# Graph attention on one Trainium2 core: attention vectors multiplied into W, the first source lines spread by products, projections and loop in one block, residual product behind the loop

## What is computed

```python
h = (x @ W).reshape(N, H, C)
a_src = jnp.einsum('nhc,hc->nh', h, att_src)
a_dst = jnp.einsum('nhc,hc->nh', h, att_dst)
logits = jax.nn.leaky_relu(a_src[src] + a_dst[dst], NEG_SLOPE)
m = jax.lax.stop_gradient(jax.ops.segment_max(logits, dst, num_segments=N))
e = jnp.exp(logits - m[dst])
s = jax.ops.segment_sum(e, dst, num_segments=N)
alpha = e / s[dst]
msg = h[src] * alpha[:, :, None]
out = jax.ops.segment_sum(msg, dst, num_segments=N).reshape(N, H * C)
out = out + x @ W_res + bias
out = (out - bn_mean) * jax.lax.rsqrt(bn_var + BN_EPS) * bn_gamma + bn_beta
return jax.nn.elu(out)
```

## Time and profile before

| | us |
|---|---|
| median of 3 runs | 3004.32 |
| lowest and highest | 3000.54, 3011.62 |
| the profiled execution's own time | 3009.49 |
| its span, first to last instruction | 3007.7 |
| block before the loop, first transpose to end | 814.4 to 849.2 |
| first logits of the loop | 868.13 |
| end of the loop | 1630.9 |
| first addition of the residual product | 1651.59 |

### The profile page before, as it was taken

One profiled execution on the slowest core, in us unless ns is written; L12 is line 12 of the kernel. 1 busy time (PEld: TensorE's weight loads), 2 busy tenths in 40 slices (PEclk: granted clock), 3 DMA queues, 4 the chain that ended last, 5 costly groups with the idle time before them and its releaser, 6 DMA issues. The chain is left out here.

```text
span 3007.7 us, 59972 instructions
## 1 busy us (share of the span) xinstructions
PE 2511.6 (84%) x19197; PEld 2068.5 (69%) x19197; DVE 2456.1 (82%) x5340; ACT 1962.6 (65%) x3958; POOL 224.6 (7%) x488
## 2 busy tenths in 40 slices
PE   0788888875449888788886599999999999999998
PEld 0555555554447666666664499988998799979997
DVE  7999999953449999899996788877887788868886
ACT  0666666640328888788885477767777677767775
POOL 3000000000000000000000111101110111101110
PEclk9999999987768899899898799999999999999999
DMA  1232332356053233533330243323333234324332
GB/s 43 76 117 107 115 131 92 133 235 164 30 148 109 108 111 121 162 120 112 122 111 27 93 149 133 140 98 130 131 143 137 91 129 149 128 78 143 147 128 86
DMA packets 87376, 355.52 MB, mean 118 GB/s; under 512 B 47453, under 2 KB 59541, under 8 KB 59796
## 3 DMA queue, kind: packets, MB, share of 16 engines
q1 hardware_dynamic: 87149, 352.59, 33.7%
HBM read 285.86 MB, written 65.67 MB: 117 GB/s over the span
## 5 line engine op out<-in xcount | busy, mean ns | idle before, releaser
L1864 ACT ACTIVATE awcol<-aturned 125x500 fp32r<-125x500 f32 (+2 forms) x652 | 373.5, 573 | 310.9 <-PE aturned L1771 307.5
L1961 DVE TENSOR_TENSOR awcol<-aturned,awcol 125x500 fp32r<-125x500 f32 (+2 forms) x652 | 427.7, 656 | 116.4 <-ACT awcol L1864 110.7
L1783 PE MATMUL asum<-awcol,vals_high 125*128 125x512 f32 (+1 forms) x1300 | 477.6, 388 | 0.0
L1366 PE MATMUL gturned<-ident,grow 125*125 125x125 f32 x2500 | 411.2, 306 | 30.1 <-ACT grow L1304 30.1
L1366 PEld LDWEIGHTS gturned<-ident,grow 125*125 125x125 f32 x2500 | 333.7, 205 | 108.5 <-issue 73.1
L1783 PE MATMUL asum<-awcol,vals_low 125*128 125x256 f32 x1300 | 402.8, 319 | 0.0
L1273 DVE SCALAR_TENSOR_TENSOR grow<-line,a_dst 125x3125 f32<-125x3125 f32 x100 | 347.5, 3475 | 38.0 <-DMA line<-lines_dram 25.6
L1304 ACT ACTIVATE grow<-grow,neg 125x3125 f32<-125x3125 f32 x100 | 290.4, 2904 | 125.0 <-DVE neg L1285 125.0
L1282 DVE CUSTOM_DVE_ANT_0 grow<-grow,bias 125x3125 f32<-125x3125 f32 x100 | 341.6, 3416 | 25.7 <-DMA bias<-bias_dram 11.6
L1344 PE MATMUL gparts<-gwcol,h_mem 125*32 125x125 f32 x5000 | 246.1, 292 | 111.4 <-ACT gwcol L1317 111.4
L1317 ACT ACTIVATE gwcol<-gturned 125x1000 f32<-125x1000 f32 x300 | 282.0, 1002 | 16.9 <-PE gturned L1366 16.7
(11 more groups left out here) (305 smaller groups left out, 4874.2 us busy)
## 6 DMA issues: line engine op xcount, KB each, us to landing
abias<-bias_dram SPq DMA_DIRECT2D x100, 1562.5 KB, 6.5
bias<-bias_dram SPq DMA_DIRECT2D x50, 1562.5 KB, 6.5
bias_dram<-lnrow SPq DMA_DIRECT2D x25, 1562.5 KB, 5.2
counts_dram<-pair SPq DMA_DIRECT2D x13, 1562.5 KB, 6.4
pair<-counts_dram SPq DMA_DIRECT2D x13, 1562.5 KB, 16.3
line<-lines_dram SPq DMA_DIRECT2D x8, 1367.2 KB
fixed<-kp SPq DMA_DIRECT2D x250, 4.0 KB, 1.7
agg<-counts_dram SPq DMA_DIRECT2D x2, 1367.2 KB
```

Of the source, the lines that this page charges most:

```text
L1366: last = pe.transpose(bank[q % RING][:, j // 4, j % 4 * T:(j % 4 + 1) * T], row[n % RING][:, t * T:(t + 1) * T], ident[0:T, 0:T])
L1783: last = pe.matmul(sum_ps[e][:, 0:n_cols], left[:, t, :], buffer[:, j * wide:j * wide + n_cols], start=(t == 0 and n == 0), stop=(t == NT ...
L1864: act.activation(operand(P, e, u, 0), turned(P, e, u), ACT.Copy).then_inc(high_copied, 1)
L1961: dve.tensor_tensor(operand(P, e, u, 1), turned(P, e, u), operand(P, e, u, 0).bitcast(FP32), ALU.subtract).then_inc(low_made, 1)
```

## The change

Line numbers of the changed kernel differ: the logits of the loop stand at 1217 instead of 1273, the transposes at 1389 instead of 1366.

- The block `pre` is gone. Its work stands at the head of the loop's block, on the loop's own three double PSUM banks used as six.
- `vcols` is gone. W is turned (128 x 128), multiplied by `att`, and the product `w_att` (128 x 8) meets `cols` directly. `att` is made on VectorE from two loads of 128 elements and the identity.
- The first two source lines (heads 0 and 1) are no longer loaded from device memory. A product whose stationary operand is one column of `w_att`, repeated 125 times, with `cols` as the moving operand gives the line on all 125 partitions; ScalarE copies it, VectorE makes the version times the slope. Heads 2 and 3 are loaded as before.
- `vals` is copied by ScalarE instead of VectorE. The load of ScalarE's Exp table stands ahead of all this.
- The product with the residual matrix is made in the block behind the loop, into seven PSUM banks, and VectorE adds it from there in seven pieces. `cols` stays for that.

```diff
@@ -1110,7 +1110,8 @@
-        res = sbo("res", [T, NT, D])
+        cols = sbo("cols2", [128, N])
+        wres = sbo("wres", [D, D])
...
-        with ExitStack() as pre:
...
-                @block.tensor
-                def _(pe):
-                    pe_turn(pe, banks, "h", h, D, ident)
-                    banks.done(pe, "h")
-                    pe.wait_ge(weights_in, 160)
-                    pe_columns(pe, banks, "vcols", w[:, :], cols)
-                    banks.done(pe, "vcols")
-                    bank = banks.fill(pe, "own", 0)
-                    for t in range(NT):
-                        last = pe.matmul(bank[0:T, 8 * t:8 * t + 8], vcols[:, t * T:(t + 1) * T], att[:, :], start=True, stop=True)
-                    last.then_inc(banks.filled, 1)
-                    pe_rows(pe, banks, "vals", [cols], [w[:, :]])
-                    pe.wait_ge(lines_made, 1)
-                    for k in range(2):
-                        pe.transpose(lines_ps[:, k, :], lines[:, k, :, :].rearrange("p h t -> p (h t)"), ident[0:T, 0:T]
-                                     ).then_inc(lines_ready, 1)
-                    pe_rows(pe, banks, "res", [cols], [wres[:, :]])
...
-                    for name, out in (("vals", vals.rearrange("p t h w -> p t (h w)")), ("res", res)):
-                        for c in range(NC):
-                            ts = tiles_of(c)
-                            bank = banks.full(dve, name, c)
-                            dve.tensor_copy(out[:, ts[0]:ts[-1] + 1, :], rows_view(bank, c, D)).then_inc(banks.read["dve"], 1)
...
+            whole_bank = [loop.enter_context(nc.psum_tensor(f"gturned{r}", [128, 2, 512], FP32)) for r in range(RING)]
+            bank = [whole_bank[r][0:T, :, :] for r in range(RING)]
+            ahead = Banks([whole_bank[r][:, j, :] for r in range(RING) for j in range(2)], sem("l2pre_filled"),
+                          {who: sem(f"l2pre_read_{who}") for who in ("act", "dve")},
+                          [("h", NC, "act"), ("w_turned", 1, "act"), ("w_att", 1, "act"), ("own", 1, "dve"), ("line0", NC, "act"),
+                           ("vals", NC, "act"), ("lines", 1, "act"), ("line1", NC, "act")])
...
-                    load_lines(0, 0)
+                    sp.dma_start(w[:, :], G["L2_gnn_W"]).then_inc(weights_in, 16)
+                    for j, name in enumerate(("L2_gnn_att_src", "L2_gnn_att_dst")):
+                        with nc.allow_non_contiguous_dma(reason="small weights"):
+                            sp.dma_start(att_in[:, j:j + 1], G[name].rearrange("h (c a) -> (h c) a", a=1)).then_inc(weights_in, 16)
+                    sp.dma_start(wres[:, :], G["L2_gnn_W_res"]).then_inc(weights_in, 16)
                     load_bias(0)
                     load_bias(1)
-                    load_lines(0, 1)
+                    ahead.done(sp, "lines", 1)
+                    sp.dma_start(G["lines_dram"].rearrange("k a p -> a k p"), lines_turned[:, :, :]).then_inc(lines_out, 16)
                     for i in range(2, NT):
                         load_bias(i)
+                    sp.wait_ge(lines_out, 16)
...
-                        dve.wait_ge(line_in[g], 2 * LANDED * (half + 1))
+                        if half:
+                            dve.wait_ge(line_in[g], 2 * LANDED)
+                        else:
+                            dve.wait_ge(line_scaled, NC * (g + 1))
...
+                    def scaled_line(g):
+                        for c, (a, z) in enumerate(CHUNKS):
+                            dve.wait_ge(line_copied, NC * g + c + 1)
+                            dve.tensor_scalar(line[g][:, 1, a:z], line[g][:, 0, a:z], SLOPE, None, ALU.mult).then_inc(line_scaled, 1)
+
+                    def heads_of(dve):
+                        m = Marks(pre_dve)
+                        src, dst = a_own[:, :, 0:HEADS], a_own[:, :, HEADS:]
+                        line_of = lambda k: lines[:, k, :, :].rearrange("p h t -> p t h")
+                        chain(dve, m, dve.tensor_reduce(in_head[:, :], ident[:, :].rearrange("p (h c) -> p h c", h=HEADS), AX.X, ALU.add))
+                        dve.wait_ge(weights_in, 64)
+                        for k in range(2):
+                            m.inc(dve.tensor_scalar(att[:, k * HEADS:(k + 1) * HEADS], in_head[:, :], att_in[:, k:k + 1], None, ALU.mult))
...
+                    heads_of(dve)
+                    scaled_line(0)
                     logits(0)
                     for n in range(UNITS):
                         maximum(n)
                         if n + 1 < UNITS:
+                            if unit(n + 1)[:3] == (0, 0, 1):
+                                scaled_line(1)
                             logits(n + 1)
 
                 @block.scalar
                 def _(act):
                     act.preload_act_table(ACT.Exp)
+
+                    def broadcast_line(g):
+                        for c, (a, z) in enumerate(CHUNKS):
+                            here = ahead.full(act, f"line{g}", c)
+                            act.activation(line[g][:, 0, a:z], here[0:T, 0:z - a], ACT.Copy).then_inc(line_copied, 1)
+                            act.wait_ge(line_copied, NC * g + c + 1)
+                            act.sem_inc(ahead.read["act"], 1)
+                    act_columns(act, ahead, "h", cols)
+                    here = ahead.full(act, "w_turned", 0)
+                    act.activation(w_turned[:, :], here[:, 0:D], ACT.Copy).then_inc(ahead.read["act"], 1)
+                    here = ahead.full(act, "w_att", 0)
+                    act.activation(w_att[:, :], here[:, 0:2 * HEADS], ACT.Copy).then_inc(ahead.read["act"], 1)
+                    broadcast_line(0)
+                    for c in range(NC):
+                        ts = tiles_of(c)
+                        here = ahead.full(act, "vals", c)
+                        act.activation(vals[:, ts[0]:ts[-1] + 1, :, :].rearrange("p t h w -> p t (h w)"), rows_view(here, c, D), ACT.Copy
+                                       ).then_inc(ahead.read["act"], 1)
+                    here = ahead.full(act, "lines", 0)
+                    act.activation(lines_turned[:, :, :], here[0:HEADS * NT, 0:2 * T].rearrange("a (k p) -> a k p", k=2), ACT.Copy
+                                   ).then_inc(ahead.read["act"], 1)
+                    broadcast_line(1)
...
+                    def broadcast_line(g):
+                        for c, (a, z) in enumerate(CHUNKS):
+                            here = ahead.fill(pe, f"line{g}", c)
+                            pe.matmul(here[0:T, 0:z - a], w_att[:, g:g + 1].broadcast_to([D, T]), cols[:, a:z], start=True, stop=True
+                                      ).then_inc(ahead.filled, 1)
+                    pe_turn(pe, ahead, "h", h, D, ident)
+                    pe.wait_ge(weights_in, 64)
+                    here = ahead.fill(pe, "w_turned", 0)
+                    pe.transpose(here[:, 0:D], w[:, :], ident[:, :]).then_inc(ahead.filled, 1)
+                    ahead.done(pe, "w_turned", 1)
+                    pe.wait_ge(pre_dve, 3)
+                    here = ahead.fill(pe, "w_att", 0)
+                    pe.matmul(here[:, 0:2 * HEADS], w_turned[:, :], att[:, :], start=True, stop=True).then_inc(ahead.filled, 1)
+                    ahead.done(pe, "w_att", 1)
+                    here = ahead.fill(pe, "own", 0)
+                    for t in range(NT):
+                        last = pe.matmul(here[0:T, 8 * t:8 * t + 8], cols[:, t * T:(t + 1) * T], w_att[:, :], start=True, stop=True)
+                    last.then_inc(ahead.filled, 1)
+                    broadcast_line(0)
+                    pe_rows(pe, ahead, "vals", [cols], [w[:, :]])
+                    pe.wait_ge(lines_made, 1)
+                    here = ahead.fill(pe, "lines", 0)
+                    for j in range(2):
+                        last = pe.transpose(here[0:HEADS * NT, j * T:(j + 1) * T], lines[:, j, :, :].rearrange("p h t -> p (h t)"), ident[0:T, 0:T])
+                    last.then_inc(ahead.filled, 1)
+                    broadcast_line(1)
+                    ahead.done(pe, "line1")
...
+            res = sb("res", [T, NT, D])
+            res_ps = [post.enter_context(nc.psum_tensor(f"l2res{c}", [T, 512], FP32)) for c in range(NC)]
+            res_ready = sem("l2res_ready")
             with nc.Block() as block:
+                @block.tensor
+                def _(pe):
+                    for c in range(NC):
+                        for j, t in enumerate(tiles_of(c)):
+                            last = pe.matmul(res_ps[c][:, j * D:(j + 1) * D], cols[:, t * T:(t + 1) * T], wres[:, :], start=True, stop=True)
+                        last.then_inc(res_ready, 1)
...
-                    chain(dve, m, dve.tensor_tensor(work[:, :, :], work[:, :, :], res[:, :, :], ALU.add))
+                    for c in range(NC):
+                        ts = tiles_of(c)
+                        here = work[:, ts[0]:ts[-1] + 1, :]
```

(21 more changed lines are left out.)

66 lines of the change are left out of this document (11 added, 55 removed).

## The result

Four runs of the changed kernel gave a median of 2975.58 us (2972.53 to 2981.03), four of the kernel before on the same chip 3007.97 (3000.54 to 3016.20). The ratio is 0.9889, with a 95% interval of 0.9869 to 0.9908: 1.1% faster, some 33 us. The sets of runs spread over 8.5 and 15.7 us. The sum of 34.4 us would be a ratio of 0.9885. The forecast of 2970 was 5.6 us too low and inside its range; 3.7 us of that is the kernel before, whose median here stands that much above the 3004.32 that the forecast started from.

What follows compares the result with a forecast made beforehand. VectorE was taken to pace the attention loop. Unit 2 starting 35.3 us earlier, less 0.9 us lost on the residual addition, gave 34.4 us saved: 2970 us from the median 3004.32, range 2959 to 2982.

Steps and rivals of the forecast that it cites:

- What bounds: Attention loop: VectorE sets the pace at 7.17 us a unit, so moving its first logits forward is worth its full length.
- Table load and columns: Turning h into columns ahead of the loop: the Exp table load now stands before ScalarE's first copy and costs nothing.
- Weights, W times attention vectors: Ahead of `own`: small loads land in time, `vcols` goes, W is turned and multiplied; `own` starts at 820.9 instead of 826.59.
- own: Ahead of the loop: 25 matmuls of the same shapes take 9.16 us as before, 9.4 at the low clock throughout.
- First line by products: Ahead of the loop: seven products take 7.0 us, between 5.5 and 11; first logits come 30.0 us earlier.
- The rival price of a doubled cost through the zero-step operand: First line's products or copies take twice their time, 7 us; part of the no-gain case at 2994 us, chance 0.04.
- Second line, ScalarE's order: Loop start: VectorE scales the second line in 2.2 us, unit 2 starts 35.3 us earlier, ScalarE's late first exponential costs nothing.
- Rival 1: Loop start: ScalarE's late start reaches VectorE at unit 3; saving only 24 to 30 us, about 2977; chance 0.20.
- Rival 2: In the loop: PE's clock is better than before, VectorE waits less; saving 38 to 46 us, about 2962; chance 0.10.
- res: Behind the loop: the residual addition in seven pieces from PSUM takes 4.4 us against 3.49, so 0.9 us lost.
- Sum: Whole kernel: 35.3 us gained at unit 2 less 0.9 lost behind the loop, 34.4 us saved.
- The rule on the clock: Ahead of the loop: gapless `own` and line products would run at full clock, saving 3 to 4 us more; not followed.

Runs made afterwards that it cites:

- e2: The changed kernel with `vcols` put back and W times the attention vectors left out: 2980.48 us, ratio 0.9908 to the kernel before.
- e4: The changed kernel with the first line's products ahead of those of `own`: 2967.30 us, ratio 0.9873 to the kernel before.
- e8: The kernel of e4 run once more, first line's products ahead of `own`: 2967.48 us, ratio 0.9857 to the kernel before.
- e5: The kernel before with only the residual product moved behind the loop and added from PSUM: 2998.79 us, ratio 0.9962 to the kernel before.
- e7: The changed kernel run again, nothing altered: 2976.29 us, ratio 0.9884 to the kernel before.
- e10: The changed kernel run again for a third profile, nothing altered: 2975.89 us, ratio 0.9890 to the kernel before.
- e3: The changed kernel with the residual product back in front of the loop, copied to SBUF by ScalarE: 2976.87 us, ratio 0.9895 to the kernel before.
- e1: The changed kernel with the lines of heads 0 and 1 loaded from device memory again: 2992.05 us, ratio 0.9937 to the kernel before.

## Why the prediction was right, and where it was off

**What bounds.** Right. The forecast rested on VectorE's first logits being worth their full length. The 34.2 us by which unit 2 moved stayed in the whole: loop and everything behind it changed by 0.3 us or less per stage. It was forecast at 35.3.

**Table load and columns.** Right, at nothing: the load ends at 812.95 and ScalarE's first copy begins at 812.96. The rule weighed there, of the Trainium skill's "ScalarE: Activation LUTs", section "What ACT_TABLE_LOAD costs", would put about 1.4 us of drain between; this trace shows 0.01 us ahead of a copy.

**Weights, W times attention vectors.** Right. The transfers were waited for until 815.19, before PE had turned its last tiles. `own` began 6.19 us behind the first transpose, against 820.9 - 814.44 = 6.5 forecast. e2 prices the edit: 3.6 us at the first logits, less than the 5.3 us by which it moves `own`.

**own.** Mis-sized: 9.16 was carried over, 10.03 measured. It was above even the 9.4 worked out for the low clock throughout, and that rate was read too fast: the 16 passes of the row's 3.00 us count those that its edges cut, and 38 in 7.70 us make 10.1. In e4 and e8 it took 5.52, in e5 6.18: the duration taken from one row held for one position of the clock's low stretch, and e5 shows that the order of PE's work ahead of it does not fix that position alone.

**First line by products.** Mis-sized by 0.7: 7.0 forecast between 5.5 and 11, 7.72 measured (7.60 and 7.71 in the repetitions e7 and e10). The reason given, coming out of the low clock, is what e4 and e8 confirm, with 5.51 at a granted clock of 1.00. The rival price of a doubled cost through the zero-step operand falls with the same number. The two terms are 1.6 us more than forecast together; 0.3 came back with the earlier start of `own`, and 0.15 as the line's products begin before the last of `own` has left PE. First logits: 24.76 against 23.7 from the first transpose.

**Second line, ScalarE's order.** Right. The scaling took 2.19 us (2.2 forecast), the first exponential began at 35.39 (35.0), unit 3 stood 7.16 us behind unit 2 with no wait. Rival 1 needed that slack to be gone; e3 shows how far: 5.2 us more reach unit 3 as 0.74. That the measured median lies near that rival's 2977 does not speak for it, since the stages that it lengthens are not longer. Its low-clock price was read a little short, too: the last 0.6 us of the 4.98 us of its 24 transposes, from 882.80 on, had a granted clock of 0.93 and more.

**Clock in the loop.** Rival 2 did not come: 13.2 us of waits for turned rows against 12.4. It is not excluded in principle. e4's profiled execution had 7.6, and its loop was 5.8 us shorter than the changed kernel's; the same program in e8 had 13.0.

**res.** The price was too high: 3.87 us for the seven pieces against 3.49, so 0.4 lost and not 0.9. Each lasts what the row used says, 0.55 to 0.69 us, which add up to 4.4; but each starts some 0.09 us before the one ahead of it has ended. What moving the product behind the loop gives at the front is worth more, as e5 shows, where it came to 11 us in all.

**Sum.** 34.4 forecast; 34.3 over the stages behind the first transpose (34.19 - 0.30 + 0.23 + 0.15), and 32.4 by medians (3007.97 - 2975.58). That the stages meet the sum to 0.1 us is in part luck. Unit 2 came 1.1 us less early than forecast, by `own` and the line; `res` gave 0.5 back, and a wait that the forecast did not name, VectorE's for `rows` behind the loop, was 0.6 us shorter (6.19 against 6.81). **The rule on the clock** was weighed rightly. "TensorE: Matmul & The Clock Gate" of the Trainium skill, section "What's actually happening", ties the gate to how busy PE has been, and would have a gapless `own` at full clock. Here `own` had no gap from 817.90 on, and the granted clock fell to 0.50 within its first 0.8 us and stayed there into the line's products. The same gapless `own` ran at 1.00 in e8, so neither the rule nor the row of one trace tells the clock of a stage.

## What to carry to other kernels

Where an engine paces a long loop and starts late, count from the first instruction of its preparation to its first full-speed unit, and look at each thing in between: here one block for two, masks loaded early, and rows that PE can spread by a product instead of a trip through device memory gave 34 us of 75. Put the work that the pacing engine waits for first in PE's order, and try more than one order: with the wide products of the line ahead of the narrow ones of `own`, the low stretch of the clock came later and was shorter, and what was left of it fell on work that VectorE does not wait for. That was worth 5.65 us more at the first logits (e4, e8). Take a PE stage's duration at both clocks into the range, since the same instructions in the same place took 6.18 and 9.16 us.

## What the hardware showed that was not expected

- The granted clock's low stretch moves between programs, and the same PE work costs more or less by it: 10.03 us for the 50 narrow passes behind 4.6 us of transposes and two small products, 8.65 behind `vcols`, 5.52 behind the line's products. Its length differs too: rows at 0.50 go on for 13.3 us in the changed kernel, 10.0 in the kernel before, 6.6 in e5 and 3.3 in e8. Within one program the time of these passes repeated to 0.1 us (10.03, 10.14 and 10.04; 5.52 and 5.52), the length of the loop did not (735.58 and 743.00).
- PE takes a single column repeated 125 times as its stationary operand at no extra cost: 5.51 us for 14 passes of 500 columns or fewer, 5.49 with a full matrix.
- Reading one 12.5 KB row from device memory to all 125 partitions, two of them to a line, took 16.0 us from the first issue to the logits in e1 and 18.9 in the kernel before. Seven products, seven copies and their scaling took 8.7 (827.78 to 836.47), about half of it at the low clock.
